# A graph-network kernel: the message stage's loads in three written-out slots, and the destination rows of attention added in PSUM

## What is computed

```python
h = jnp.maximum(_layernorm(x, axis=-1), 0.0)
x = x + _L0_gnn_ref(h, W_l, b_l, W_r, b_r, att, bias, src, dst)      # attention
    m = x_l[s] + x_r[d]; m = where(m >= 0, m, 0.2 * m); e = einsum('ehc,hc->eh', m, att)
    out = segment_sum(softmax over d of e * x_l[s], d) + bias
h = jnp.maximum(_layernorm(x, axis=-1), 0.0)
x = x + _L1_gnn_ref(h, edge_attr_20, edge_weight, src, dst, ...)     # messages
    Wij = (shifted_softplus(f_ij @ Wf1 + bf1) @ Wf2 + bf2) * rcut_ij
    agg = segment_sum((h @ W_in2f)[idx_j] * Wij, idx_i)
    out = shifted_softplus(agg @ Wo1 + bo1) @ Wo2 + bo2
```

## Time and profile before

| | |
|---|---|
| runs | 3313.77, 3317.54 and 3329.19 us, median 3317.54 us |
| profiled execution | 3332.83 us, of it the span 3331.0 us |
| busy share of the span | PE 76%, PE's weight loads 53%, DVE 74%, ACT 66%, POOL 58% |
| granted clock of PE, mean | 0.908 of full speed |

### The profile page before, as it was taken

One profiled execution on the slowest core, in us unless ns is written; L12 is line 12 of the kernel. 1 busy time (PEld: TensorE's weight loads), 2 busy tenths in 40 slices (PEclk: granted clock), 3 DMA queues, 4 the chain that ended last, 5 costly groups with the idle time before them and its releaser, 6 DMA issues. The chain is left out here.

```text
span 3331.0 us, 58371 instructions
## 1 busy us (share of the span) xinstructions
PE 2544.2 (76%) x16674; PEld 1760.3 (53%) x16674; DVE 2454.0 (74%) x6275; ACT 2194.7 (66%) x4803; POOL 1916.5 (58%) x1633
## 2 busy tenths in 40 slices
PE   6776777788887877787886777777777777758887
PEld 5554555444443444444444665666555565547776
DVE  7554555678887877887787778777878778737776
ACT  6655666667777777777775555555555555549998
POOL 2564555267766666766752777777777777720000
PEclk9877899989999999999998889788899899979999
DMA  7665566333333333333333666666666666679998
GB/s 239 241 229 187 212 215 214 118 117 130 127 126 116 130 116 129 118 128 116 124 102 102 117 116 116 115 113 117 119 117 119 116 117 118 114 261 404 424 422 350
DMA packets 323596, 558.99 MB, mean 168 GB/s; under 512 B 135552, under 2 KB 211828, under 8 KB 285794
## 3 DMA queue, kind: packets, MB, share of 16 engines
q1 hardware_dynamic: 226290, 448.50, 40.1%
q0 software_dynamic: 97200, 109.30, 16.6%
HBM read 324.12 MB, written 242.20 MB: 170 GB/s over the span
## 5 line engine op out<-in xcount | busy, mean ns | idle before, releaser
L665 POOL DMA_INDIRECT sum_dram<-b_sum,b_at x392 | 641.1, 1636 | 233.3 <-issue 117.2
L589 POOL DMA_INDIRECT a_xd<-in_x,index x344 | 361.5, 1051 | 162.4 <-issue 100.0
L580 POOL DMA_INDIRECT a_xs<-in_x,index x344 | 364.5, 1060 | 146.8 <-issue 101.6
L598 POOL DMA_INDIRECT x_dram<-a_xo,index x196 | 211.4, 1079 | 290.7 <-DVE a_xo L900 191.7
L1330 PE MATMUL bank<-wl,turned 128*128 128x128 f32 x1568 | 263.8, 319 | 74.4 <-ACT turned L1106 54.4
L802 DVE TENSOR_TENSOR d_x<-bank,d_x 128x512 f32<-128x512 f32 x196 | 134.7, 687 | 239.0 <-remote 142.6
L1330 PEld LDWEIGHTS bank<-wl,turned 128*128 128x128 f32 x1568 | 222.5, 219 | 134.4 <-ACT turned L1106 89.5
L1109 ACT ACTIVATE d_n<-d_x,stat_d_shift,stat_d_rstd 128x128 f32<-128x128 f32 x686 | 283.3, 485 | 0.2 <-DVE stat_d_shift L701 0.2
L1453 PE MATMUL bank<-b_rows,b_same 128*128 128x128 bf16 x4704 | 279.9, 219 | 0.6 <-ACT b_sum L1246 0.6
L1486 PE MATMUL bank<-wo,f_ssp_out 128*128 128x128 f32 x1568 | 225.3, 287 | 55.9 <-DVE f_ssp_out L1055 51.9
L1453 PEld LDWEIGHTS bank<-b_rows,b_same 128*128 128x128 bf16 x4704 | 265.1, 98 | 0.6 <-issue 0.6
(11 more groups left out here) (191 smaller groups left out, 7025.7 us busy)
## 6 DMA issues: line engine op xcount, KB each, us to landing
d_x<-in_x SPq DMA_DIRECT2D x49, 1024.0 KB
x_dram<-d_x SPq DMA_DIRECT2D x49, 1024.0 KB
out<-d_x SPq DMA_DIRECT2D x49, 1024.0 KB, 7.6
sum_dram<-zero SPq DMA_DIRECT2D x48, 1024.0 KB
d_x<-x_dram SPq DMA_DIRECT2D x45, 1024.0 KB, 12.0
d_n<-sum_dram SPq DMA_DIRECT2D x25, 1024.0 KB, 9.1
x_end_dram<-a_xo SPq DMA_DIRECT2D x98, 256.0 KB
b_x<-x_end_dram SPq DMA_DIRECT2D x98, 256.0 KB
```

Of the source, the lines that this page charges most:

```text
L580: pool.indirect_dma_start(a_xs[t % DEPTH][:, j * F:(j + 1) * F], None, x, column(t, j)).then_inc(gathered[t % GSEM], 16)
L589: pool.indirect_dma_start(a_xd[t % DEPTH][:, j * F:(j + 1) * F], None, x, column(t, TILES + j)).then_inc(gathered[t % GSEM], 16)
L598: pool.indirect_dma_start(x1_dram, column(t, 2 * TILES + j), a_xo[t % 4][:, j * F:(j + 1) * F], None, bounds_check=bound, oob_is_err=False ...
L665: pool.indirect_dma_start(sum_dram, bass.IndirectOffsetOnAxis(ap=b_at[s][:, j:j + 1], axis=0), b_sum[s][:, j * F:(j + 1) * F], None, compu ...
```

## The change

In the attention stage TensorE adds `a_xd` into the same bank with a product by the unit matrix, and ScalarE reads the sum out as `a_xo`, with the waits that VectorE had; VectorE's addition is gone. In the message stage the loops on the chip are gone on every engine; `b_x`, `b_fa`, `b_goes`, `b_w` and `b_src` have three slots (`DB`), all five loads of a chunk count on one semaphore `b_ld`, and are issued together. `b_end`, `sidx` and `b_col` are not copied any more: their readers take the columns out of the tables `ends`, `index` and `columns`. Half the slots of `a_xd` move in SBUF, so that `f_pre` lies behind the larger tiles.

```diff
+DB = 3
...
-            b_x = at2("b_x", [P, TILES * F])
-            b_fa = at2("b_fa", [P, TILES * 32])
-            b_goes = at2("b_goes", [P, C], BF16)
...
+            b_x = [at(f"b_x{i}", [P, TILES * F]) for i in range(DB)]
+            b_fa = [at(f"b_fa{i}", [P, TILES * 32]) for i in range(DB)]
+            b_goes = [at(f"b_goes{i}", [P, C], BF16) for i in range(DB)]
...
-        b_x_ld = sems("b_x_ld"); b_fa_ld = sems("b_fa_ld"); b_goes_ld = sems("b_goes_ld"); b_w_ld = sems("b_w_ld")
-        b_src_ld = sems("b_src_ld"); sidx_ld = sems("sidx_ld"); b_col_ld = sems("b_col_ld")
-        x1_scattered = sems("x1_scattered"); added = sems("added")
+        b_ld = sems("b_ld", DB)
+        x1_scattered = sems("x1_scattered", DB); added = sems("added")
...
+        def loaded(t):
+
+            return 16 * 5 * (t // DB + 1)
+
+        def scattered(t):
+
+            return 16 * sum(TILES - EARLY[1 - u % 2] for u in range(t % DB, t + 1, DB))
...
-            def load_rows_b(k, u, t0):
-
-                s = u % 2
-                t = 2 * k + u
-                if t0 >= 2:
-                    sp.wait_ge(b_y_ready, t - 1)
+            def load_b(t):
+
+                s = t % DB
+                if t >= DB:
+                    for sent in (b_y_ready, b_fa_turned, b_msg_ready, b_same_ready):
+                        sp.wait_ge(sent, t - DB + 1)
+                        sp.sem_inc(sync_step, 1)
+                    sp.wait_ge(x1_scattered[s], scattered(t - DB))
                     sp.sem_inc(sync_step, 1)
-                    sp.wait_ge(b_masked, t - 1)
-                    sp.sem_inc(sync_step, 1)
-                    sp.wait_ge(x1_scattered[s], late(s) * turn(k, u - 2))
-                    sp.sem_inc(sync_step, 1)
-                sp.dma_start(b_x[s][:, :], x1_end_dram[bass.ds(NC - 1 - t, 1), :, :].rearrange("o p f -> (o p) f")).then_inc(b_x_ld[s], 16)
-                sp.dma_start(b_end[s][:, :], ends[:, bass.ds(TILES * (NC - 1 - t), TILES)]).then_inc(b_x_ld[s], 16)
-                sp.dma_start(sidx[s][:, :], index[:, bass.ds(12 * (NC - 1 - t) + 8, 4)]).then_inc(sidx_ld[s], 16)
-                if t0 >= 2:
-                    sp.wait_ge(b_fa_turned, t - 1)
-                    sp.sem_inc(sync_step, 1)
+                c = NC - 1 - t
+                sp.dma_start(b_x[s][:, :], x1_end_dram[c:c + 1, :, :].rearrange("o p f -> (o p) f")).then_inc(b_ld[s], 16)
                 sp.dma_start(b_fa[s][:, :].rearrange("p (j r) -> p j r", j=TILES)[:, :, 0:RBF],
-                             attr_dram[bass.ds((NC - 1 - t) * C, C), :].rearrange("(j p) r -> p j r", p=P)).then_inc(b_fa_ld[s], 16)
...
-            def step_b(k, u, t0, ahead=True):
-
-                s = u % 2
-                t = 2 * k + u
-                if ahead:
-                    load_rows_b(k, u + 1, t0 + 1)
-                if t0 >= 2:
-                    sp.wait_ge(b_msg_ready, t - 1)
-                    sp.sem_inc(sync_step, 1)
-                sp.dma_start(b_goes[s][:, :], goes_dram[bass.ds(NC - 1 - t, 1), :].broadcast_to([P, C])).then_inc(b_goes_ld[s], 16)
-                sp.dma_start(b_w[s][:, :], weight_dram[bass.ds(NC - 1 - t, 1), :].broadcast_to([P, C])).then_inc(b_w_ld[s], 16)
-                if t0 >= 2:
-                    sp.wait_ge(b_at_ready, t - 1)
-                    sp.sem_inc(sync_step, 1)
-                sp.dma_start(b_src[s][:, :], src_dram[bass.ds(NC - 1 - t, 1), :].broadcast_to([P, C])).then_inc(b_src_ld[s], 16)
-                sp.dma_start(b_col[s][:, :], columns[:, bass.ds(8 * (NC - 1 - t), 8)]).then_inc(b_col_ld[s], 16)
-
...
-            load_rows_b(0, 0, 0)
...
+                             attr_dram[c * C:c * C + C, :].rearrange("(j p) r -> p j r", p=P)).then_inc(b_ld[s], 16)
+                sp.dma_start(b_goes[s][:, :], goes_dram[c:c + 1, :].broadcast_to([P, C])).then_inc(b_ld[s], 16)
+                sp.dma_start(b_w[s][:, :], weight_dram[c:c + 1, :].broadcast_to([P, C])).then_inc(b_ld[s], 16)
+                sp.dma_start(b_src[s][:, :], src_dram[c:c + 1, :].broadcast_to([P, C])).then_inc(b_ld[s], 16)
+
+            for t in range(NC):
+                load_b(t)
...
             def scatters(k, u):
-                s = u % 2
-                pool.wait_ge(sidx_ld[s], 16 * turn(k, u))
-                pool.wait_ge(b_x_ld[s], 32 * turn(k, u))
+                t = 2 * k + u
+                pool.wait_ge(b_ld[t % DB], loaded(t))
                 pool.sem_inc(pool_step, 1)
-                for j in range(EARLY[1 - s], TILES):
-                    pool.indirect_dma_start(x1_dram, bass.IndirectOffsetOnAxis(ap=sidx[s][:, j:j + 1], axis=0),
-                                            b_x[s][:, j * F:(j + 1) * F], None,
-                                            bounds_check=bound, oob_is_err=False).then_inc(x1_scattered[s], 16)
+                for j in range(EARLY[1 - t % 2], TILES):
+                    pool.indirect_dma_start(x1_dram, column(NC - 1 - t, 2 * TILES + j),
+                                            b_x[t % DB][:, j * F:(j + 1) * F], None,
+                                            bounds_check=bound, oob_is_err=False).then_inc(x1_scattered[t % DB], 16)
...
-            for u in range(4):
-                scatters(0, u)
-                if u >= 2:
-                    adds(0, u - 2, first=u == 2)
-            with pool.Fori(2, HALF) as k:
-                for u in range(2):
-                    scatters(k, u)
-                    adds(k, u - 2)
+            for t in range(NC):
+                scatters(t // 2, t % 2)
+                if t >= 2:
+                    adds(t // 2, t % 2 - 2, first=t == 2)
...
-                if back:
-                    dve.wait_ge(out_turned, t - 1)
-                    if t >= 6:
-                        dve.wait_ge(end_stored[s], 16 * ((t - 6) // 2 + 1))
-                        dve.wait_ge(early_scattered[s], 16 * EARLY[s] * ((t - 6) // 2 + 1))
-                    dve.tensor_tensor(a_xo[(t - 2) % 4][:, :], bank[6 + s][:, :], a_xd[(t - 2) % DEPTH][:, :], ALU.add).then_inc(x1_ready, 1)
...
-                dve.wait_ge(b_x_ld[s], 32 * turn(k, u))
+                t = 2 * k + u
+                dve.wait_ge(b_ld[t % DB], loaded(t))
                 if t0 >= 2:
                     dve.wait_ge(b_norm, 2 * k + u - 1)
-                dve.tensor_tensor(b_y[s][:, :], b_x[s][:, :], bo_row[:, :], ALU.subtract).then_inc(b_y_ready, 1)
+                dve.tensor_tensor(b_y[s][:, :], b_x[t % DB][:, :], bo_row[:, :], ALU.subtract).then_inc(b_y_ready, 1)
...
-                        last = dve.tensor_scalar(b_same[o][:, j, :], b_src[o][:, :], b_col[o][:, j:j + 1], None, ALU.is_equal)
+                        last = dve.tensor_scalar(b_same[o][:, j, :], b_src[c][:, :], columns[:, 8 * (NC - t) + j:8 * (NC - t) + j + 1], None, ALU.is_equal)
...
-            for u in range(4):
-                step_b(0, u, u, mid=u >= 1, back=u >= 2)
-            with dve.Fori(2, HALF - 1) as k:
-                for u in range(2):
-                    step_b(k, u, 4 + u)
-            step_b(HALF - 1, 0, 4)
-            step_b(HALF - 1, 1, 5, ahead=False)
-            step_b(HALF, 0, 4, ahead=False, front=False)
-            step_b(HALF, 1, 5, ahead=False, front=False, mid=False)
+            for t in range(NC + 2):
+                step_b(t // 2, t % 2, t, ahead=t + 1 < NC, front=t < NC, mid=1 <= t <= NC, back=t >= 2)
...
                     act.activation(a_hs[:, :], bank[0][:, :], ACT.Copy)
                     act.wait_ge(turned_dst, t + 1)
                     act.activation(a_hd[t % 3][:, :], bank[1][:, :], ACT.Relu).then_inc(h_dst, 1)
+                if t >= 2:
+                    act.wait_ge(out_turned, t - 1)
+                    if t >= 6:
+                        act.wait_ge(end_stored[s], 16 * ((t - 6) // 2 + 1))
+                        act.wait_ge(early_scattered[s], 16 * EARLY[s] * ((t - 6) // 2 + 1))
+                    act.activation(a_xo[(t - 2) % 4][:, :], bank[6 + s][:, :], ACT.Copy).then_inc(x1_ready, 1)
                 if mid:
...
@@ -1371,6 +1324,7 @@
                     pe.matmul(to[:, :], ones3[:, 0:P], bias_d3[:, :, :].rearrange("k j f -> k (j f)"), start=True, stop=False)
                     for j in range(TILES):
                         pe.matmul(to[:, j * F:(j + 1) * F], a_hd[c % 3][:, j * P:(j + 1) * P], wl[:, :], start=False, stop=False)
+                    pe.matmul(to[:, :], ident[:, :], a_xd[c % DEPTH][:, :], start=False, stop=False)
                     pe.wait_ge(att_out, c + 1)
                     for j in range(TILES):
                         last = pe.matmul(to[:, j * F:(j + 1) * F], a_o[s][:, j * P:(j + 1) * P], ident[:, :],
```

More of the change, by code:

```diff
@@ L144, in gnn @@
         stat_e = stat("stat_e", 4 * TILES, 2)
-        sidx = [sb(f"sidx{i}", [P, 4], I32) for i in range(2)]
         turned = [sb(f"turned{i}", [P, 512]) for i in range(2)]
@@ L1189, in _ @@
             norms_dst(0)
-            for t in range(NC + 1):
+            for t in range(NC + 2):
                 step_a(t)
```

65 lines of the change are left out of this document (19 added, 46 removed).

## The result

The changed kernel takes 3557.1 us in the median of four runs (3551.6 to 3559.5), the kernel before 3323.4 (3313.8 to 3330.3): ratio 1.070 (95% interval 1.067 to 1.074), 234 us slower. The forecast was 3467 us, the range 3375 to 3545, counted from 3317.5 us, the median of the first three runs of the kernel before. The direction was right, the size was not, and the time lies above the range.

What follows compares the result with a forecast made beforehand. The prediction saw rings of waits: TensorE and ScalarE in attention, loads and VectorE in the message stage. Attention +116 and message +33 gave +149 us on 3317.5, so 3467 us, range 3375 to 3545.

Steps and rivals of the forecast that it cites:

- How long five loads take ... I take 5.7.: Message stage: 5.7 us from b_same's end to b_y, making the step 11.65 us against 11.31, +33 us.
- The ring: Message stage: b_same ends, five loads are issued, all land, b_y runs, and on to b_same again; 11.65 us a step.
- The 5.95 us of the other part: Message stage: VectorE's time from b_y to the end of b_same, taken between 6.2 and 5.7 us.
- The lower end: Message stage: five loads take 4.95 us, 2.2 us of issue plus 2.75 us for b_end's load; step 10.9 us, -40 us.
- The upper end: Message stage: five loads take 6.9 us, their bytes at 136 GB/s; step 12.85 us, +149 us.
- Sum for attention: +116 us.: Attention stage: matmul 0.85 plus ScalarE read 0.50 minus hole 0.14 gives 1.2 us a step, times 97.
- I take these stalls as unchanged: Attention stage: ScalarE's unexplained longer waits for transposes, 21 times and 78.8 us in 1000 us, stay as before.
- rival 3: Attention stage: the unexplained stalls take the new work in, so attention costs nothing; 3351 us, chance 0.05.
- Rival 1: Message stage: the load ring is good and gains 40 us, attention as forecast; 3394 us, chance 0.15.
- rival 2: Attention stage: VectorE bounds it, so each step gives back 0.68 us, 66 us in all; 3285 us, chance 0.09.
- Rival 4: Message stage: the loads are at the upper bound, +149 us; 3583 us, chance 0.06.
- some 2: Start of the message stage: the first b_y waits for five loads instead of two, some 2 us once.

Runs made afterwards that it cites:

- experiment 4: Changed kernel with four load slots in place of three; 3092.4 us against 3011.5 for the kernel before, ratio 1.027.
- experiment 5: Changed kernel with its load ring opened in two versions, on another slower chip; 3401.5 and 3370.9 us, changed kernel 3609.9, kernel before 3362.1.
- second version of experiment 5: Changed kernel with one wait moved, so that only b_src waits for b_same; 3370.9 us, ratio 1.003 to the kernel before.
- experiment 6: Kernel before with the new matmul alone, VectorE copying the sum out; 3077.3 us against 3006.2, ratio 1.023.
- experiment 3: Kernel before with only the message stage's loops written out on all five engines; 3001.8 us against 3011.5, ratio 0.998.
- first version of experiment 5: Changed kernel with a semaphore for each load, so b_y waits for b_x only; 3401.5 us, ratio 1.013 to the kernel before.

## Why the prediction was wrong, by its own steps

**"How long five loads take ... I take 5.7."** This is the term that put the time outside the range. The ring was the right one and stands in every row: b_same's end, five issues, five landings, b_y. From the end of b_same to b_y are 6.7 to 9.2 us in 92 steps of the trace after, 7.7 in the mean, where the prediction had 5.7 and a bound of 6.9. The 5.95 us of the other part came out at 5.7. Experiments 4 and 5, each of which opens this ring by another means (a slot more, b_y waiting for one load, four of five loads sent early), take away 208 to 239 us, all of the +184 and the gain that lay behind it.

Both ends of my bound failed by what they left out. The lower end added a lone 2 KB load's 2.75 us to the issue times, as if the large loads ahead of the last one took no time. The upper end divided the bytes by 136 GB/s and counted nothing for the time in which no byte of the loads moves. The step shown divides so, in windows from the end of b_same to the first packet of the loads, to their last packet, to b_y, and to the end of the next b_same:

```profile
2403.77:2404.88 1.11, 0.49 (x3) 0.49 (x4) 1.11 (x3) 0.72 (x3) 1.11 (x1) 0.50 0.00 0
2404.88:2410.74 5.86, 5.86 (x49) 4.90 (x49) 2.35 (x3) 3.05 (x5) 4.95 (x4) 0.69 0.83 188
2410.74:2411.16 0.42, 0.42 (x12) 0.42 (x10) 0.00 (x0) 0.00 (x0) 0.42 (x1) 1.00 1.04 118
2411.16:2416.89 5.73, 2.68 (x29) 1.71 (x26) 5.52 (x21) 2.50 (x7) 2.78 (x4) 1.00 0.19 31
```

By the packet records of 80 steps the means are 0.2 us to the first issue, 0.95 us from there to the first packet, 6.1 us of packets and 0.4 us from the last packet to b_y. The packets alone take longer than the 5.7 us that I took for everything. The 6.9 us would have covered them; the 1.5 us around them are what the upper bound lacked. While they move, the DMA engines are 87% busy, 25% of their time with the packets of GpSimd's queue, so in this part of the step they are near their limit. The stage's mean share of 0.52 hides that, because they are nearly idle in the other part. How short the five loads would be without GpSimd's traffic, no run shows. In the second version of experiment 5 b_src is not alone either: between its issue and b_y, 624 kB of loads move in the mean of 80 steps, and only 262 kB of them are its own, so it stands behind the loads sent before it.

**"Sum for attention: +116 us."** Each term was right: 0.85 us for the matmul, 0.28 for the read where I had 0.36, 1.14 against 1.2 in a free step, and +95 us in four runs of the edit alone on the faster chips. On the recorded chip the stage grew by 34 us only. The step that failed is "I take these stalls as unchanged". The mean step over the free one, 11.81 - 10.12 = 1.69 us before, is 12.16 - 11.25 = 0.91 us after; 97 x 0.78 = 76 us less for what is over the free steps. ScalarE's waits for a_hd with no releaser fell from 78.8 us to this:

```profile
ACT a_hd L1110 <- remote: 41.0, 8, 6.0
```

A long step of before, in windows that follow one another:

```profile
818.00:822.00 4.00, 4.00 (x27) 2.86 (x26) 3.26 (x5) 2.94 (x7) 3.08 (x4) 1.00 0.49 169
822.00:826.00 4.00, 0.08 (x1) 0.00 (x0) 1.33 (x5) 0.00 (x0) 1.96 (x3) 0.82 0.76 290
826.00:831.00 5.00, 4.23 (x5) 1.85 (x6) 3.37 (x13) 3.68 (x8) 3.79 (x4) 0.50 0.11 33
```

TensorE and ScalarE stand still for 4 us, in this step while 290 GB/s move, and then TensorE works at a granted clock of 0.50, its lower level of 1.2 GHz. With the change the stage's clock is 0.98 against 0.94, so by my estimate from these two means (each 0.01 missing is 2% of the time at 0.50) some 4% of the time is at the lower level instead of 12%. That is what rival 3 foretold, to which I had given 0.05, at two thirds of its size; the chip of experiment 5 shows it again (+0.45 us a step). It is seen only in the two pairs of traces and not shown by an experiment of the attention edit alone on such a chip. Why the stops shrink, what makes them, and whether it is the new work that takes their place, stays open.

**The rivals.** Rival 1 (a good load ring) and rival 2 (VectorE bounds attention) are refuted: b_y's wait grew, and VectorE's share fell from 81% to 73% while the step became longer. The Trainium skill's rule ("Perfetto Trace Analysis", Identifying the Most-Contended Engine) would have chosen rival 2; the trace does not agree: with VectorE relieved by 74 us of busy time in 1000, the step grew. By experiment 6 the work that moved to TensorE and ScalarE accounts for the growth of a free step; VectorE was not on the ring. Rival 4 (the loads at the upper bound) is what the message stage did, and beyond: +184 us where it had +149. Its total of 3583 us is above the result because the attention stage cost 82 us less than its sum. That the result lies between the forecast and this rival is luck: the sum had 151 us too little in the message stage and 82 us too much in attention, and the two errors stood against each other.

**What was costed at nothing.** The written-out loops (10 us faster if anything, experiment 3) and the tables read on chip cost nothing, as predicted. The first b_y's longer wait was 4 us against "some 2".

## What to carry to other kernels

Before several loads are put on one semaphore, look for the wait that releases their slots last and the wait that needs them first: if they lie so close that the loads have no cover between them, all loads stand in the ring, and the time of the last one counts, not that of the first. One wait moved behind four of the five issues was worth 239 us of 3610 here. When no row shows how long a burst of loads takes, bytes over a rate price only the time in which its packets move; add what lies between the issue and the first packet and between the last packet and the reader (1.5 us here, with the first issue). A share averaged over a step says nothing of a part of it. When mean steps are longer than free ones, price an edit on the free step and keep a wide range for the rest.

## What the runs showed of the hardware

- Chips differ by 10% on the same kernel (3003 to 3011 us on four, 3323 and 3362 us on two). The record doesn't have the same chip at two times, so whether it is the chip or its state at that time isn't shown. The difference lies in the first stage (first a_o at 474 against 644 us) and in the attention stage (10.35 us a step against 11.81 and 12.06), and hardly in the message stage (11.22 against 11.31). The same edit cost 3.2% on the one kind; on the other it showed as about 1% within the whole change.
- Five loads of 959 kB on one queue, beside GpSimd's adds, kept the DMA engines 87% busy for 6.1 us at 184 GB/s in all. The first packet came 0.95 us after the first issue, and the reader started 0.4 us after the last packet (means of 80 steps after).
- The first add of a step took 2.55 us on GpSimd when it started 0.34 us ahead of the five loads' issue, the next three 1.55 to 1.57. The burst alone doesn't do that: with the same five loads sent together, but at another moment of GpSimd's step, the mean of all adds was 1593 ns (first version of experiment 5) and 1582 ns (experiment 4), against 1808 ns in the changed kernel. Why the moment matters isn't shown.
- On the recorded chip TensorE and ScalarE stood together for 1.5 to 4.6 us 27 times in the attention stage before and 12 times after. Behind the twelve stops of before that lasted over 3 us, TensorE's granted clock was 0.50 to 0.59 for the next 4 us. On a faster chip the same code did so three times, once for 9.9 us (experiment 3).
